# Layernorm folded into the K and V weights and into ScalarE's evictions; GpSimd sums all three thirds of the softmax weights

## What is computed

```python
def _layer_norm(x, gamma, beta):
    mu = jnp.mean(x, axis=-1, keepdims=True)
    var = jnp.mean(jnp.square(x - mu), axis=-1, keepdims=True)
    return (x - mu) * jax.lax.rsqrt(var + LN_EPS) * gamma + beta
a = _layer_norm(audio_kv, ln_gamma, ln_beta)            # (32, 375, 512)
Q = (hidden_states @ Wq.T).reshape(B, Tt, HEADS, HEAD_DIM).transpose(0, 2, 1, 3)
K = (a @ Wk.T).reshape(B, Ta, HEADS, HEAD_DIM).transpose(0, 2, 1, 3)
V = (a @ Wv.T).reshape(B, Ta, HEADS, HEAD_DIM).transpose(0, 2, 1, 3)
scores = jnp.einsum('bhtd,bhsd->bhts', Q, K) * scale
scores = jnp.where(mask, scores, jnp.float32(-jnp.inf))
attn = jax.nn.softmax(scores, axis=-1)
out = jnp.einsum('bhts,bhsd->bhtd', attn, V)
out = out.transpose(0, 2, 1, 3).reshape(B, Tt, D) @ Wo.T
return hidden_states + jnp.tanh(gate) * out
```

## Time and profile before

| | |
|---|---|
| median of three runs | 1026.55 us |
| profiled execution: its own time, its span | 1022.71 us, 1020.5 us |
| mean granted TensorE clock | 0.987 |
| PE busy | 989.4 us, 97% |
| DVE busy | 748.4 us, 73% |
| POOL busy | 719.8 us, 71% |
| ACT busy | 661.7 us, 65% |
| DMA | 102.26 MB, 100 GB/s mean |

### The profile page before, as it was taken

How to read it: one execution, slowest core, us unless ns; L and a number is a source line. 1 busy time by engine, 2 the same in 40 slices (tenths; PEclk the granted TensorE clock), 3 DMA queues, 4 the chain that set the end, 5 groups by cost and what they waited for, 6 DMA issues and landing times.

```text
span 1020.5 us, 32130 instructions
## 1 busy us (share of the span) xinstructions
PE 989.4 (97%) x11665; PEld 831.9 (82%) x11665; DVE 748.4 (73%) x1414; ACT 661.7 (65%) x1364; POOL 719.8 (71%) x977
## 2 busy tenths in 40 slices
PE   9997999999999999999999999999999999999975
PEld 8896887888888888878888888888888888888863
DVE  6640388887877777787777787778887787877773
ACT  3313577766766766777666776667776676776662
POOL 1447878787777777787777787777878777775221
PEclk9999999999999999999999999999999999999997
DMA  9653433333334344433433443444333334331111
GB/s 298 195 160 68 124 93 83 88 100 105 81 104 106 101 109 107 108 88 88 103 85 96 110 105 102 109 107 110 85 95 102 90 89 112 82 81 30 31 36 41
DMA packets 83252, 102.26 MB, mean 100 GB/s; under 512 B 29024, under 2 KB 65888, under 8 KB 83200
## 3 DMA queue, kind: packets, MB, share of 16 engines
q10 hardware_dynamic: 24652, 56.60, 20.5%
q1 hardware_dynamic: 58548, 44.94, 17.1%
HBM read 91.34 MB, written 10.19 MB: 99 GB/s over the span
## 4 chain that ended last, share of the span: by engine, by line
PE 48%; DMA 26%; DVE 18%; issue 3%; POOL 1%; ACT 1%; SPq 1%; DVEq 0%; POOLq 0%; ACTq 0%
PE bank L766 33%; DMA row_max<-rmax 12%; DMA x<-row_max 10%; DVE rmax L714 7%; PE sbank L860 5%; PE bank L876 5%; DVE shared_f L724 4%; DVE bank L704 2%; DVE stats L673 2%; PE bank L782 2%; DVE top L701 1%; PE bank L885 1%; PE bank L881 1%; DMA row_stats<-row_stat 1%; PE sbank L782 1%
## 5 line engine op out<-in xcount | busy, mean ns | idle before, releaser
L766 PE MATMUL bank<-shared_r,w_k 128*128 128x376 f32 x1536 | 300.0, 344 | 5.8 <-ACT shared_f L622 5.7
L766 PE MATMUL bank<-w_v,shared_r 128*125 128x512 f32 x1152 | 284.8, 396 | 0.0
L766 PEld LDWEIGHTS bank<-shared_r,w_k 128*128 128x128 f32 x1536 | 259.6, 189 | 27.7 <-issue 21.1
L600 ACT ACTIVATE shared_f<-shared_f 125x448 f32<-125x448 f32 x384 | 201.4, 586 | 92.3 <-DVE shared_f L724 92.0
L766 PEld LDWEIGHTS bank<-w_v,shared_r 128*125 128x125 f32 x1152 | 213.3, 186 | 45.3
L714 DVE TRANSPOSE_TENSOR_REDUCE rmax<-shared_f 128x14 f32<-128x448 f32 x384 | 216.4, 614 | 36.5 <-ACT shared_f L569 36.4
L569 ACT ACTIVATE shared_f<-sbank,mask_b 125x448 f32<-125x448 f32 x384 | 215.7, 636 | 25.7 <-PE sbank L860 25.6
L724 DVE TENSOR_TENSOR shared_f<-shared_f,bank 125x448 f32<-125x448 f32 x384 | 215.4, 616 | 4.5
L452 POOL TENSOR_TENSOR shared_f<-shared_f 125x448 f32<-125x448 f32 x128 | 150.3, 1174 | 93.7 <-ACT shared_f L600 91.4
L413 POOL TENSOR_TENSOR cn<-cn,stat_bc 128x375 f32<-128x375 f32 x128 | 117.7, 952 | 91.3 <-DMA cn<-in_ctxT 76.8
L701 DVE TENSOR_REDUCE top<-x 128x14 f32<-128x168 f32 x128 | 55.9, 437 | 138.9 <-DMA x<-row_max 138.7
(11 more groups left out here) (65 smaller groups left out, 901.6 us busy)
## 6 DMA issues: line engine op xcount, KB each, us to landing
cn<-in_ctxT ACTq DMA_DIRECT2D x30, 750.0 KB, 6.0
rows<-in_ctx ACTq DMA_DIRECT2D x28, 720.0 KB
stat_bc<-row_stats ACTq DMA_DIRECT2D x29, 375.0 KB, 4.3
x<-row_max SPq DMA_DIRECT2D x128, 84.0 KB
xy<-in_x SPq DMA_DIRECT2D x32, 224.0 KB, 3.9
out<-xy SPq DMA_DIRECT2D x32, 224.0 KB
shared_f<-in_xT SPq DMA_DIRECT2D x7, 896.0 KB, 9.2
rows<-in_ctx SPq DMA_DIRECT2D x4, 720.0 KB
```

Of the source, the lines that this page charges most:

```text
L600: act.activation(prob[0:SP_, (r - 3) % NB, j, :], prob[0:SP_, (r - 3) % NB, j, :], ACT.Exp, scale=SCALE).then_inc(exp_done, 1)
L766: last = pe.matmul(dst, l, m, start=(start and k == 0), stop=(stop and k == len(pairs) - 1))
```

## The change

gamma and the mean go into the weights: Wk and Wv (transposed, rows are input columns) are multiplied by gamma row by row, and the mean over all 512 rows is subtracted from each output column. Multiplied with such a weight, a context row gives what the centred row would. What is left of the normalisation, one over the deviation of a context row, is a factor of a partition in the evictions of the scores and of V (`scale=rstd`). beta adds a constant to each K row, which falls out of the softmax, and a constant to V, which is carried through Wo and added to x before the result (`gbo`, `add_bias`).

So `center`, `divide`, `affine`, the store and the spread load of the statistics go, and the context is split as it comes from DRAM. ctxT is loaded by chunk into eight buffers, one load of 187.5 KB a slot. The rows for the statistics are loaded with row 125j+p on partition p (three pieces of 2 KB for each partition, where one of 6 KB was). The Q stage gets new work: VectorE sums the scaled weights (`scaled_sum`) and centres them (`centre`), TensorE takes means (`mean`) and carries beta through Wv and Wo, GpSimd multiplies Wv by beta and Wo by the result (`products`); the Q groups are ordered by output bank, so that a bank comes free for the means. VectorE splits the first context. GpSimd adds all three thirds of the softmax weights, and L881 goes.

```diff
-        rows_v = ctx.rearrange("b (p j) d -> b p j d", j=ST)
+        rows_v = ctx.rearrange("b (j p) d -> b p j d", j=ST)
-        def load_ctx(queue, i, c):
-            queue.dma_start(cn[:, c % 2, :, :], ctxT_v[i * 2 + c, :, :, :]) \
-                .then_inc(ld_ctx[c % 2], 16)
+        def load_ctx(queue, i, m):
+            if behind(i, LOOP, m - 2 * KT + 1):
+                wait_apart(queue, c_done, i * LOOP + (m - 2 * KT + 1))
+            queue.dma_start(cn[:, m % (2 * KT), :], ctxT_v[i * 2 + m // KT, :, m % KT, :]) \
+                .then_inc(ld_ctx[m % (2 * KT)], 16)
 # SyncE, start
-            load_ctx(sync, 0, 0)
             load_rows(sync, 0, 1)
-            store_stats(0, 0)
-            load_stats(sync, 0, 0)
-            with sync.Fori(2, GROUPS // 2) as i:
-                for g in range(2):
-                    wait_apart(sync, xr_done, i * 2 + (g - 1))
-                    load_xT(i, g)
+            for m in range(KT):
+                load_ctx(sync, 0, m)
+            for n in range(4, GROUPS):
+                sync.wait_ge(xr_done, n - 1)
+                load_xT(n // 2, n % 2)
 # GpSimd
-                then(pool.tensor_tensor(row_stat[:P, 1, :], tmp[:P, :], rs0[:P, :], ALU.mult))
+                pool.tensor_tensor(rstd[:P, c % 2, :], tmp[:P, :], rs0[:P, :], ALU.mult) \
+                    .then_inc(rstd_done, 1)
+            def products(dst, raw, factor, s_step, s_ready):
+                for k in range(KT):
+                    to = dst if k == 0 else part
+                    if k > 1:
+                        pool.wait_ge(s_step, 2 * k - 1)
+                    pool.tensor_scalar(to[:, :], raw[:, k, :], factor[:, k:k + 1], None, ALU.mult) \
+                        .then_inc(s_step, 1)
+                    if k > 0:
+                        pool.wait_ge(s_step, 2 * k)
+                        pool.tensor_tensor(dst[:, :], dst[:, :], part[:, :], ALU.add) \
+                            .then_inc(s_step if k < KT - 1 else s_ready, 1)
                 pool.tensor_tensor(psum[0:SP_, :], prob[0:SP_, q, 0, :], prob[0:SP_, q, 1, :],
+                                   ALU.add).then_inc(sum_half, 1)
+                wait_apart(pool, sum_half, i * LOOP + (r - 2))
+                wait_apart(pool, exp_done, i * (LOOP * ST) + ((r - 3) * ST + 3))
+                pool.tensor_tensor(psum[0:SP_, :], psum[0:SP_, :], prob[0:SP_, q, 2, :],
                                    ALU.add).then_inc(sum_done, 1)
-                if live(i, 2, c + 2, B) and not first_two(i, c + 2):
-                    if u == 0:
-                        center(i, c + 2, (0, 1, 2, 3))
-                    if u == 1:
-                        divide(i, c + 2, (0, 1, 2, 3))
-                    if u == 2:
-                        affine(i, c + 2, (0, 1, 2, 3))
+                if u == 1 and live(i, 2, c + 1, B) and not first_two(i, c + 1):
+                    row_statistics(i, c + 1)
+                if u == 0 and live(i, 2, c - 2, B):
+                    add_bias(i, c - 2)
 # ScalarE
                                    sbank[0:SP_, :, T * j:T * j + T], ACT.Identity,
-                                   bias=mask_b[0:SP_, c % 2, j:j + 1]).then_inc(s_out, 1)
+                                   bias=mask_b[0:SP_, c % 2, j:j + 1],
+                                   scale=rstd[0:SP_, c % 2, j:j + 1]).then_inc(s_out, 1)
-                if u == 3:
-                    if live(i, 2, c + 3, B) and behind(i, 2, c + 1):
-                        load_stats(act, i, c + 3)
-                    if live(i, 2, c + 3, B) and not first_two(i, c + 3):
-                        wait_apart(act, c_done, i * LOOP + (c + 2) * KT)
-                        load_ctx(act, i, c + 3)
-                if u == 2 and live(i, 2, c + 5, B) and behind(i, 2, c + 2):
-                    load_rows(act, i, c + 5)
+                if live(i, LOOP, r + 11, SLOTS) and behind(i, LOOP, r + 12 - 2 * KT):
+                    load_ctx(act, i, r + 11)
+                if u == 2 and live(i, 2, c + 3, B) and behind(i, 2, c + 1):
+                    load_rows(act, i, c + 3)
 # VectorE
+            def scaled_sum(w, raw, dst):
+                dve.wait_ge(ld_w[w], 16)
+                dve.tensor_scalar(dst[:, :], raw[:, 0, :], gam[:, 0:1], None, ALU.mult) \
+                    .then_inc(sum_ready[w], 1)
+                for k in range(1, KT):
+                    dve.wait_ge(sum_ready[w], k)
+                    dve.scalar_tensor_tensor(dst[:, :], raw[:, k, :], gam[:, k:k + 1], dst[:, :],
+                                             ALU.mult, ALU.add).then_inc(sum_ready[w], 1)
+            def centre(w, raw):
+                dve.wait_ge(mean_mm[w], 1)
+                if w == "v":
+                    dve.wait_ge(b_ready, 1)
+                for k in range(KT):
+                    dve.scalar_tensor_tensor(raw[:, k, :], raw[:, k, :], gam[:, k:k + 1],
+                                             mean_bank[w], ALU.mult, ALU.subtract) \
+                        .then_inc(centred[w], 1)
+            x_group(1)
+            statistics(0, 0)
+            dve.wait_ge(ld_const, 48)
+            scaled_sum("k", raw_k, sum_k)
+            x_group(2)
+            scaled_sum("v", raw_v, sum_v)
+            x_group(3)
+            centre("k", raw_k)
+            weight_lo("k", raw_k, wk)
+            centre("v", raw_v)
+            x_group(4)
 # TensorE
+            def q_group(n):
+                pe.wait_ge(xr_done, n + 1)
+                for m in range(KT):
+                    if n > 1:
+                        pe.wait_ge(q_out, (n - 2) * KT + m + 1)
+                    if n == 2 and m == 3:
+                        pe.wait_ge(centred["k"], KT)
+                    if n == 3 and m == 2:
+                        pe.wait_ge(bv_out, 1)
+                    if n == 3 and m == 3:
+                        pe.wait_ge(centred["v"], KT)
+                    if n == 5 and m == 3:
+                        pe.wait_ge(bo_out, 1)
+            first_q_group()
+            q_group(1)
+            mean("k", sum_k, KT)
+            q_group(2)
+            mean("v", sum_v, 2 * KT)
+            beta_through_v()
+            q_group(3)
+            q_group(4)
+            beta_through_o()
-                for h in range(HC):
-                    pe.matmul(bank[PB][HD * h:HD * h + HD, T:2 * T], ones[0:SP_, :],
-                              prob[0:SP_, (r - 3) % NB, ST - 1, T * h:T * h + T], start=True, stop=False)
```

284 lines of the change are left out of this document (145 added, 139 removed).

## The result

The changed kernel takes 1008.14 us (median of 4 runs, 1007.71 to 1008.93); the kernel before, on the same chip, 1025.91 (1023.06 to 1027.88). The ratio is 0.9839, 95% interval 0.9806 to 0.9872: 1.6% or 17.8 us less, clear of noise but under 2%. The forecast was 991 for 1026.55, 35.5 less (33.7 by its sum), and its range ended at 1008. The profiled execution took 1007.96 us, its span 1006.2.

A forecast was written before the change was run, and what follows sets the result against it. TensorE, busy throughout the loop, was taken as the bound. -24.3 - 2.0 - 7.9 + 0.5 = -33.7 us took the profiled 1022.7 to 989.0, and half the median's 3.8 offset made 991; range 982 to 998, widened to 1008.

The forecast's parts named there:

- (1): TensorE's loop slot: dropping L881's eight matmuls takes 7.00 us to 6.81, 24.3 us over 128 slots.
- (2): GpSimd in the loop: second addition ends 2.2 us behind last exp; exps needed 1.6 us ahead of weighted sum.
- (3): Loop: exchange of maxima 12.3 plus VectorE 15.9, 28.3 us a batch; the change makes it 10.4 + 15.9 = 26.3.
- A: Loop: VectorE and the exchange of maxima take over at 28 us a batch; near 1013; chance 0.08.
- B: Loop: a ctxT load in every slot slows each exchange, 29.5 us a batch; slower, 1053; chance 0.05.
- (4): ScalarE's evictions in the loop read a second pointer: 93 ns each, 1.4 us a batch, hidden.
- (5): DMA queues of SyncE and ScalarE: four loads a batch instead of one hold nothing behind them; costed at nothing.
- The stalls: Loop: of 5.7 us of waits for exps outside the one at the end, 2.0 gained (0 to 3).
- The start: Before the first scores: old stalls -4.15 and -8.4, means and beta +3.2, new stall +1.5; net -7.9 us.
- Rival C: The start does not gain: two centrings each hold TensorE 4 to 5 us and it cools; 1000; chance 0.10.
- The end: Behind the loop: three evictions and part of an addition cost +0.5 us (0 to 2).
- Rival D: Loop: the second addition is late by 1.1 us each batch, 35 us, all gains eaten; 1024; chance 0.03.

The follow-up runs named there:

- e8_extra_add: `e1_pool_order` with the third chunk added a second time on GpSimd in every slot (denominators wrong): 1089.42 us, ratio 1.0656.
- e10_vector_4: `e1_pool_order` with four unused VectorE reductions ahead of the store of the maxima, once a batch: 991.84 us, ratio 0.9701.
- e9_vector_2: `e1_pool_order` with two unused VectorE reductions ahead of the store of the maxima, once a batch: 992.81 us, ratio 0.9711.
- e3_third_on_pe: `e1_pool_order` with the third chunk's denominator matmuls back on TensorE and its addition off GpSimd: 1013.52 us, ratio 0.9919.
- e1_pool_order: The changed kernel with GpSimd's second products moved ahead of the row statistics of batch 1: 992.43 us, ratio 0.9716.
- e1_again: `e1_pool_order` run again, unchanged, beside the runs that build on it: 991.39 us, ratio 0.97.
- e4_before_third_on_pool: The kernel before with only the second addition put on GpSimd and L881 gone, layernorm still on GpSimd: 1057.7 us, ratio 1.0364.

## Why the prediction was right or wrong

**The slot, (1): right.** 6.81 us instead of 7.00, and 7.00 again when it is undone. The loop is 24.3 us shorter, the number of the forecast, but 1.2 of it are stalls, which the forecast had as a term of its own (2.0): -24.3 and -2.0 together came out as -24.3.

**The latency on GpSimd, (2): the mechanism right, the place of the shortage not.** The second addition starts 0.28 to 0.34 behind the first and takes 1.17, as costed, and GpSimd's waits hold TensorE for 2.8 us only. The working has two slips: 1.17 + 0.2 + 1.17 - 0.5 is 2.04 and not 2.2, and the slot would be late by 0.42 - 0.19 - 1.37 = -1.1; with the plus sign that stands there it would be -0.8. Neither moves the forecast. But the text looked for what makes the exps late in the tightest slot. In the changed kernel the exps stand some 3.3 us ahead of their weighted sum, and the slot with row statistics has the least room (the sum is ready 0.5 us ahead on the mean, 1.5 in the others) because GpSimd arrives late from its own queue, as `e8_extra_add` shows.

**The ring, (3): wrong as a sum.** What it was to bring did come: the exps are early, and VectorE's waits for the maxima fell from 138.7 to 8.3 us. But its terms are not what they were taken for. "Exchange 12.3 + VectorE 15.9 = 28.3, as long as TensorE's batch" was read from one store to the store of the same slot in the next batch. In a periodic schedule any such walk is one period long, 28.0, whoever sets the period, so the length alone is no evidence of a bound. The 10.0 of the changed kernel is near the 10.4 of the forecast by luck: it is the time at which VectorE comes by, and with the store 2.9 us later it was 7.1 (`e10_vector_4`). The store's landing follows the loads ahead of it and not its own issue. And 2.9 us put into the ring cost nothing. So rivals A and B, which lived on the ring, had no ground in the changed kernel. For the kernel before it stays open whether the exchange was level with TensorE. VectorE did wait for the maxima 56 times there and worked from 518.55 to 534.48 without a pause, the loop had 3.0 us of stalls, and no run lengthens or shortens the exchange in that kernel alone. Nor is it settled what ended those waits; the bytes, the pieces and the order in which ctxT's load and the maxima's load are issued all changed together.

By the Trainium skill, "DMA: Bandwidth & Descriptors", section "Queues, rings and completion order", a queue's packet is drained before the engine turns, which made pieces of 2 KB look better for the store. The runs show no such effect (5.82 us with 2 KB, 5.36 with 6 KB). That the store waits for loads ahead of it is shown by `e9_vector_2` and `e10_vector_4`; whether packets are the reason, no run here shows.

**Evictions, (4): right.** 724 instead of 636 ns, 88 more for 93 forecast, hidden. **Queues of DMAs, (5): right** in that they held nothing on ScalarE in the loop. **The stalls, 2.0 us to be gained:** the 3.0 us of before are gone (`e3_third_on_pe` has none), but the sum of thirds brought 1.8 of its own; net 1.2.

**The start: wrong, and nearly the whole miss.** Forecast -7.9, measured +9.3, 17.2 us apart; by the spans the change brought 14.3 for a forecast of 33.7, 19.4 apart, and the other 2.0 are the loop's. What was costed came out: the old stalls before the fifth Q group and the second K are gone, a mean of 512 columns takes 0.46 us of TensorE (26.19 to 26.65; 0.9 forecast), the stall in Q group 2 was 1.94 for 1.5, with about 1.4 of slow clock behind it that was not costed. What failed is the term for `beta_through_o`, the third of the "three mean matmuls": 0.9 us for the work, and nothing for a wait, without a reason. Its matmul was costed on TensorE, but nobody asked for the arrival of its input: the second `products` on GpSimd, queued behind `row_statistics(0, 1)`, which waits for VectorE's statistics, which are queued behind the low parts of the weights. 13.6 us idle and some 2 at low clock. All three positions can be read in the code. With that one line moved, the start is -7.2 (`e1_pool_order`; -5.5 in `e1_again`) for the -7.9 of the forecast, which so was the price of that order and not of this. That the two medians, 992.4 and 991.4, lie on its 991 is in part luck, because the kernel before read 1021.6 and 1021.3 beside them and not 1026.55. By the ratios, 0.9716 and 0.97 of 1026.55, it would be 997 and 996, 5 to 6 us above the forecast; 2.0 of them lie in the loop (-24.3 for -24.3 and -2.0). Rival C had the right place (the start does not gain) and the wrong mechanism: centring holds TensorE 1.9 us, not 4 to 5.

Moving it is not free: beside VectorE, GpSimd's product of seven instructions takes 16.4 us (42.62 to 59.0) instead of 12.3 (63.29 to 75.6), one multiplication up to 3.7 us instead of 1.56. This agrees with the Trainium skill, "SBUF — State Buffer", section "Who interferes with whom", on which the prediction drew for VectorE alone, and from which it took the cost to stay in the start; the 2.43 us of L758 in `e4_before_third_on_pool` lie in the loop. It still ends 1.7 us before it is due.

**The end: right**, +0.75 for +0.5.

**Rival D** was rightly dismissed for this kernel and wrongly priced: what it describes costs not the lateness of one addition but the push of the whole queue and the slow matmuls behind the gap, 98 us in `e8_extra_add` for 1.45 more a slot. That its time would come back once TensorE is late did not hold there either.

## What to carry to other kernels

For each new instruction on the bounding engine, write down who makes each of its inputs, and walk that engine's queue backwards to its last wait, through every engine on the way. A cyclic path read from a steady loop is one period long by construction. Lengthen it (a few extra instructions will do) and look whether the time grows, and whether the added time is still there at the end of the path. A time from a store to the first use says how long an exchange takes only if the user waited for it. An engine that is busy for 83% of the span can be the bound, and work taken off it is what lets the next step pay. And a gap on TensorE is to be priced with the slow matmuls behind it, here 1.6 to 2.6 us for a gap of 2.2. Compare medians of different sessions by their ratios to a kernel that ran beside each.

## What the runs showed of the hardware

- A gap of 2.16 us on TensorE in a fully busy loop was followed by a granted clock of 0.76 on the mean of the next 7 us; in the changed kernel TensorE was idle for 1.2 us in all between 112 and 300 (busy 186.78 of 188.00), and the clock stayed at 1.00:

```profile
112.00:300.00 188.00, 186.78 (x2141) 155.55 (x2141) 150.50 (x285) 141.37 (x278) 117.06 (x146) 1.00 0.35 85
```

- A plain float32 matmul of 512 columns stands in the trace as two matmuls, which end 1.02 us after their start; the next work starts after 0.46.
- The same GpSimd multiplication of 128x512 took 1.56 us alone (66.68 in the changed kernel) and up to 3.7 beside VectorE's two-input work in SBUF (53.86 in `e1_pool_order`), but 1.62 beside such work in one case (27.21 in the changed kernel).
- A small store (21 KB) issued behind a 720 KB load on another queue landed at a time that its own issue did not set: the load that waits for the store was issued 6.8 us behind the large one, whether the store followed that by 0.9, 2.25 or 3.8 us (`e1_again`, `e9_vector_2`, `e10_vector_4`).
